# A scan-and-feed-forward layer on one core: the softplus rounding error moves from TensorE to GpSimd, three products instead of four per half, 29 idle products instead of 32, and a new order of work

## The chip, the cores and the metric

The kernel runs on one core of a Trainium2 chip. The metric is the device time of one execution in microseconds (us); three runs of the kernel before took 560.64, 560.69 and 561.02 us, median 560.69. The core has a matrix engine (TensorE, PE), a vector engine (VectorE, DVE), an activation engine (ScalarE, ACT), a general engine (GpSimd, POOL) and a queue for transfers (SyncE, SP). Each runs its own instruction list in order; semaphores make one wait for another.

## The reference

Eight sequences ("images" below) of 512 positions and width 128 go through a Mamba layer and a gated feed-forward layer, each with a residual and a layer norm. Cut to what matters:

```python
h = x * rsqrt(mean(x*x) + 1e-5) * norm_w
xs, res = split(h @ in_proj_w.T)                    # 256 wide each
u = silu(causal_conv4(xs) + conv_b)
delta, Bm, Cm = split(u @ x_proj_w.T, [64, 80])     # 64, 16, 16
delta = softplus(delta @ dt_proj_w.T + dt_proj_b)
# for each of 256 channels and 16 states n, along the 512 positions:
state = exp(delta * A[n]) * state + (delta * u) * Bm[n]
y = sum_n state[n] * Cm[n] + u * D
x = layernorm(x + (y * silu(res)) @ out_proj_w.T + x)
x = layernorm(x + (silu(x @ wg.T) * (x @ wu.T)) @ wd.T)   # hidden 384
```

## The kernel before

**Tiling.** An image's 256 channels times 16 states are 32 groups of 128 rows by 512 positions; 4 groups make a quad, so an image has 8 quads (0 to 7). Quads 0 to 3 belong to channel half 0, quads 4 to 7 to half 1. For each group, ScalarE makes the decay `exp(delta * A)` in one of three PSUM banks (`exp_decay`, L731, up to three groups ahead of the scan, one bank each), and VectorE scans it with `prod` (L1196). GpSimd makes `prod` for a whole quad at once (`multiply`, L1018), into one of two buffers; quad q may be overwritten only when quad q-2 is scanned. After the fourth scan of a quad VectorE weighs the states with the C row (`weigh`, L1206), which TensorE has spread over the partitions in `c_ps` (`spread_c`, "C" in the plan, L484). In five quads of an image (`SHARED`) GpSimd weighs the first group (`weigh_first`, L1040), so that VectorE's weighing covers three groups, not four. TensorE then sums the states into `y_ps` (`sum_states`, "S", L500; at quads 0 and 4 with the skip product L498 ahead of it), and VectorE may not start quad q before the sum of quad q-2 is done.

**What lies beside the scans.** While image k is scanned, the input side of image k+1 ("ins": h, conv, `res`, `xd`, softplus, B rows) and the output side of image k-1 ("outs": projection, first norm, feed-forward, second norm) are worked off in the same loop. TensorE's order is written out by hand: `PLAN` has a list for each quad; "Fname" is an idle product (`stir`, L508, 128x256 on `x_all`, its result is never read) into the bank of the job that it names. `BANK` gives each job one of three PSUM banks; a job and an idle product wait until the bank's job before was taken. `ACT_AT`, `DVE_AT` and `POOL_AT` say after which scan step (0 to 31) or quad the other engines do their part. ScalarE's decay n+1 always comes ahead of its other work of step n.

**The softplus.** `softplus(z)` is `relu(z) + ln(1 + e)` with `e = exp(-|z|)`, and the rounding error of `1 + e` is put back. ScalarE makes `z_abs`, `z_pos` (relu), `z_e`, `z_w = 1 + e`, `z_wm = 1 - z_w` and `z_ln = Ln(1 + e)`; TensorE adds four of them up for each half with products by the identity (job "d": `z_e`, `z_wm`, `z_pos`, `z_ln`; L545 to L551), and ScalarE copies the sum out as `delta` (`take_delta`, L769). SyncE then spreads `delta` and `du = delta * u` (GpSimd, `scale_u`, L1035) over the partitions with 16 transfers for each image. Ln and Silu need other function tables than Exp and Tanh, so ScalarE loads a table ahead of and behind each of them.

**Start and end.** Iteration -1 prepares image 0, iterations 0 to 7 scan an image each (7 has no ins and so none of the idle products named after ins jobs), and `tail` finishes the last image, with idle products of its own (`STIR_TAIL`).

## Time and profile before

| | before |
|---|---|
| median of 3 runs | 560.69 us |
| the profiled execution, its span | 562.91 us, 561.1 us |
| PE busy | 522.8 us (93%) |
| DVE busy | 495.8 us (88%) |
| ACT busy | 385.8 us (69%) |
| POOL busy | 414.2 us (74%) |
| mean granted TensorE clock | 0.963 of 2.4 GHz |

The span runs from the first to the last instruction; the execution's own time is 1.8 us more. A busy TensorE includes the idle products. Most of the span is eight nearly equal stretches, one for each image scanned; each starts with the first scan of the image. A 512-wide fp32 product shows as two records, an idle product as two records, a sum of a quad as eight.

### The profile page before, as it was taken

The page shows a single profiled execution, that of the slowest core. Times are in us where ns is not written, and L with a number is a line of the kernel's source. Part 1 is how long each engine was busy: PE and PEld are TensorE (multiplying, and loading weights), DVE is VectorE, ACT ScalarE, POOL GpSimd, SP SyncE. Part 2 cuts the span into 40 slices and gives each one's busy share as a digit, 9 for nine tenths or more (in the row PEclk, how much of TensorE's full clock was granted, in tenths as well). Part 3 has the DMA queues.
Part 4 walks back from the last instruction along what each step waited for, and adds up shares of the span by engine and source line. Part 5 has one row for each costly group of instructions (what it writes and reads, how often), then busy time and mean ns, then how long its engine had stood idle before and what let it go on. Part 6 is the DMA issues. An engine that isn't in the chain of part 4 may idle for free.

```text
span 561.1 us, 7049 instructions
## 1 busy us (share of the span) xinstructions
PE 522.8 (93%) x2161; PEld 272.9 (49%) x2161; DVE 495.8 (88%) x559; ACT 385.8 (69%) x625; POOL 414.2 (74%) x212
## 2 busy tenths in 40 slices
PE   8989998999999999999999999999999997668695
PEld 6444444545564536545564536544564534433363
DVE  5867789998999999999999999999999999998863
ACT  3676896599478975699478974799478974554231
POOL 8769677996579874996589874996589874996310
PEclk9979999999999999999999999999999999759798
DMA  8062305600624032700624032600634042700000
GB/s 224 9 151 56 96 8 143 151 0 2 150 59 111 1 73 78 167 4 0 151 62 108 0 82 70 169 0 0 150 63 106 0 90 60 168 2 0 0 20 19
DMA packets 27391, 39.29 MB, mean 70 GB/s; under 512 B 3832, under 2 KB 10072, under 8 KB 27360
## 3 DMA queue, kind: packets, MB, share of 16 engines
q1 hardware_dynamic: 25168, 38.38, 28.7%
q10 hardware_dynamic: 2192, 0.55, 0.5%
q8 instruction: 13, 0.21, 0.2%
q14 instruction: 18, 0.15, 0.1%
HBM read 3.27 MB, written 2.10 MB: 10 GB/s over the span
## 4 chain that ended last, share of the span: by engine, by line
PE 74%; DVE 9%; issue 6%; ACT 5%; POOL 2%; DMA 1%; SPq 1%; POOLq 0%; DVEq 0%; ACTq 0%
PE dense_ps L508 18%; PE y_ps L500 9%; PE dense_ps L526 9%; PE dense_ps L577 7%; DVE state L1196 6%; PE dense_ps L584 3%; PE c_ps L484 3%; PE dense_ps L528 2%; PE dense_ps L533 2%; PE dense_ps L545 2%; PE y_ps L498 2%; PE dense_ps L547 2%; PE dense_ps L551 2%; PE dense_ps L549 2%; PE dense_ps L541 2%
## 5 line engine op out<-in xcount | busy, mean ns | idle before, releaser
L1018 POOL TENSOR_TENSOR prod<-du_rep,b_rep 128x2048 f32<-128x2048 f32 x63 | 286.0, 4544 | 71.9 <-ACT b_rep L778 50.0
L1196 DVE TENSOR_TENSOR_SCAN state<-decay_ps,prod 128x512 f32<-128x512 f32 x256 | 298.9, 1207 | 17.3 <-ACT decay_ps L731 10.6
L731 ACT ACTIVATE decay_ps<-delta_rep,a_neg 128x512 f32<-128x512 f32 x252 | 170.0, 689 | 71.8 <-DVE state L1196 71.6
L1206 DVE TENSOR_TENSOR state<-state,c_ps 128x1536 f32<-128x1536 f32 (+1 forms) x63 | 122.8, 1949 | 19.0 <-PE c_ps L484 14.8
L508 PE MATMUL dense_ps<-x_all,ident 128*128 128x256 f32 x476 | 121.8, 398 | 5.6 <-ACT z_pos L757 3.6
L508 PEld LDWEIGHTS dense_ps<-x_all,ident 128*128 128x128 f32 x476 | 88.5, 195 | 48.4 <-issue 15.6
L500 PE MATMUL y_ps<-state,gather 128*32 128x512 f32 x504 | 70.8, 635 | 4.6 <-DVE state L1206 4.6
L526 PE MATMUL dense_ps<-h_t,tap_t 128*128 128x512 f32 x128 | 58.4, 598 | 0.9 <-ACT h_t L789 0.9
L1040 POOL TENSOR_TENSOR state<-state,c_rep 128x512 f32<-128x512 f32 x40 | 51.4, 1285 | 4.3 <-ACT c_rep L774 4.2
L484 PE MATMUL c_ps<-bc,pick 64*128 64x512 f32 x64 | 31.6, 493 | 8.4 <-DVE state L1206 8.4
L526 PEld LDWEIGHTS dense_ps<-h_t,tap_t 128*128 128x128 f32 x128 | 23.2, 189 | 30.5 <-issue 29.4
L1035 POOL TENSOR_TENSOR z_wm<-z_ln,u 128x512 f32<-128x512 f32 x15 | 19.2, 1279 | 23.9 <-ACT z_ln L769 23.8
L484 PEld LDWEIGHTS c_ps<-bc,pick 64*128 64x128 f32 x64 | 12.3, 192 | 36.5 <-issue 22.1
L500 PEld LDWEIGHTS y_ps<-state,gather 128*32 128x32 f32 x504 | 10.1, 110 | 38.1 <-issue 31.7
L577 PE MATMUL dense_ps<-x_t,up_t 128*128 128x512 f32 x42 | 22.2, 651 | 5.3 <-DVE g_act L1271 4.4
L778 ACT ACTIVATE b_rep<-dense_ps 128x512 f32<-128x512 f32 x31 | 17.6, 594 | 9.2 <-PE dense_ps L541 8.9
L577 PE MATMUL dense_ps<-x_t,gate_t 128*128 128x512 f32 x42 | 22.9, 627 | 0.0
L731 ACT ACT_TABLE_LOAD x16 | 20.5, 1283 | 2.4 <-PE decay_ps L477 2.1
L584 PE MATMUL dense_ps<-down_t,g_act 128*128 128x128 f32 x168 | 19.9, 275 | 0.0
L584 PEld LDWEIGHTS dense_ps<-down_t,g_act 128*128 128x128 f32 x168 | 19.3, 192 | 0.0
L769 ACT ACTIVATE z_ln<-dense_ps 128x512 f32<-128x512 f32 x14 | 8.3, 590 | 16.0 <-PE dense_ps L551 16.0
L856 ACT ACTIVATE y_out<-dense_ps 128x512 f32<-128x512 f32 x7 | 4.2, 597 | 21.9 <-PE dense_ps L584 21.9
(201 smaller groups left out, 691.3 us busy)
## 6 DMA issues: line engine op xcount, KB each, us to landing
du_rep<-z_wm SPq DMA_DIRECT2D x64, 256.0 KB, 5.0
delta_rep<-z_ln SPq DMA_DIRECT2D x64, 256.0 KB, 4.5
out_dram<-y_out SPq DMA_DIRECT2D x7, 256.0 KB, 4.7
state<-L_attn_in_proj_w_in ACTq DMA_DIRECT2D x1, 256.0 KB, 3.9
x_all<-L_attn_x_in SPq DMA_DIRECT2D x1, 256.0 KB, 4.2
state<-L_ffn_w_gate_in SPq DMA_DIRECT2D x1, 192.0 KB, 10.0
state<-L_ffn_w_up_in SPq DMA_DIRECT2D x1, 192.0 KB, 3.5
state<-L_ffn_w_down_in SPq DMA_DIRECT2D x1, 192.0 KB, 4.3
```

The lines of the kernel that those rows point to most:

```text
L484: mm(c_ps[:, :], pick[R:, CHUNKS + quad % CHUNKS, :], bc[it.now][R:, :], start=True, stop=True).then_inc(c_ready, 1)
L500: last = mm(y_ps[DB * c:DB * c + DB, :], gather[:, :], state[quad % 2][:, c, :], start=False, stop=(q == CHUNKS - 1), tile_position=(0, DB ...
L508: mm(it.ps(name)[:, 0:2 * P], ident[:, :], x_all[:, 0:2, :], start=True, stop=True)
L526: last = mm(ps[:, :], tap_t[:, n, j, :], h_t[:, j:j + T], start=(j == 0), stop=(j == TAPS - 1))
L577: last = mm(ps[:, :], (gate_t if kind == "gate" else up_t)[:, n, :], x1_t[:, :], start=True, stop=True)
L584: last = mm(ps[:, i * P:(i + 1) * P], g_act[:, b, i * P:(i + 1) * P], down_t[:, b, :], start=False, stop=(b == HID - 1 and i == TILES - 1))
L731: A(decay_ps[n % DECAYS][:, :], decay_ps[n % DECAYS][:, :] if spread_first else delta_rep[:, h, c, :], ACT.Exp, scale=a_neg[:, col:col + 1 ...
L1018: TT(prod[quad % 2][:, :, :], du_rep[:, h, :, :], b, ALU.mult).then_inc(prod_ready, 1)
L1035: TT(du[:, h, :], delta[:, h, :], u[it.next][:, h, :], ALU.mult).then_inc(du_ready, 1)
L1040: TT(state[quad % 2][:, 0, :], state[quad % 2][:, 0, :], c_rep[:, quad % CHUNKS, :], ALU.mult).then_inc(share_ready, 1)
L1196: dve.tensor_tensor_scan(state[n // BLOCKS % 2][:, n % BLOCKS, :], decay_ps[n % DECAYS][:, :], prod[n // BLOCKS % 2][:, n % BLOCKS, :], 0. ...
L1206: TT(state[quad % 2][:, mine, :], state[quad % 2][:, mine, :], c_ps[:, :].unsqueeze(1).broadcast_to([P, BLOCKS - mine.start, T]), ALU.mult ...
```

## The change

GpSimd gets a new step `error_of`: `z_wm = z_e + z_wm`, once for each half. TensorE's job "d" then adds three arrays instead of four, in the order `z_pos`, `z_wm`, `z_ln`. The tables of the order are written anew: the plan has 29 idle products instead of 32, other banks, other steps, and GpSimd takes over the first group in quads 0, 1, 4, 5, 6 instead of 1, 2, 4, 5, 6.

```diff
@@ the plan and the tables (a few of the lines)
-        PLAN = [["Fh", "Fh", "Fh", "Fh", "Fh", "Fh", "Fh", "Fh", "C", "Fh", "S", "h"],
-                ["proj", "xs0", "C", "S", "xs1"],
+        PLAN = [["Fh", "Fh", "Fh", "Fh", "Fh", "Fh", "Fh", "h", "S", "C"],
+                ["Fxs0", "Fxs0", "xs0", "proj", "C", "xs1", "S", "res0", "res1"],
...
-        ACT_AT = {"hx": 1, "y": 4, "h": 3, "r1": 7, "silu": 9, "xd": 13, "x1n": 11, "z": (16, 17), "x1": 16,
-                  "ze": 17, "zw": 19, "zwm": 20, "ln": 21, "gate": (20, 22, 23), "b": (25, 28, 31, 31), "down": 29,
-                  "d": (23, 25), "c": 2}
+        ACT_AT = {"hx": 0, "y": 5, "h": 0, "r1": 5, "silu": 9, "xd": 12, "x1n": 12, "z": (13, 15), "x1": 14,
+                  "ze": 15, "zw": 16, "zwm": 18, "ln": 19, "gate": (19, 19, 21), "b": (24, 28, 31, 31), "down": 28,
+                  "d": (20, 24), "c": 2}
...
-        POOL_AT = {1: [], 2: ["C1"], 3: ["norm1", "C2"], 4: ["low"], 5: ["C4"], 6: ["scale0", "C5"], 7: ["C6"],
-                   8: ["scale1", "norm2"]}
+        POOL_AT = {1: ["C0"], 2: ["C1"], 3: ["norm1"], 4: [], 5: ["low", "error0", "error1", "C4"],
+                   6: ["C5", "scale0"], 7: ["C6", "scale1"], 8: ["norm2"]}
         STIR_HEAD = {"h": 12, "xs0": 3, "du0": 5}
-        STIR_TAIL = {"S": 7, "x1": 6, "gate0": 0}
+        STIR_TAIL = {"S": 8, "x1": 5, "gate0": 1}
@@ TensorE, job "d"
-                    it.wait(pe, z_step, 4, 1, 3)
-                    mm(ps[:, :], ident[:, :], z_e[:, n, :], start=True, stop=False)
-                    it.wait(pe, wm_ready, 1, 1, 1)
+                    it.wait_taken(pe, f"z{n}")
+                    mm(ps[:, :], ident[:, :], z_pos[:, n, :], start=True, stop=False)
+                    it.wait(pe, err_ready, HALVES, 0, n + 1)
                     mm(ps[:, :], ident[:, :], z_wm[:, n, :], start=False, stop=False)
-                    it.wait_taken(pe, f"z{n}")
-                    mm(ps[:, :], ident[:, :], z_pos[:, n, :], start=False, stop=False)
                     it.wait(pe, ln_ready, 1, 1, 1)
                     last = mm(ps[:, :], ident[:, :], z_ln[:, n, :], start=False, stop=True)
@@ GpSimd
+            def error_of(it, h):
+                it.wait(pool, z_step, 4, 1, 3)
+                it.wait(pool, wm_ready, 1, 1, 1)
+                TT(z_wm[:, h, :], z_e[:, h, :], z_wm[:, h, :], ALU.add).then_inc(err_ready, 1)
```

TensorE's list at the start of an image, before, from the sum of the last image's quad 7 (L500) to the first idle products of quad 2; L519 is job h, L556 and L560 are proj, L526 a conv half (xs0, xs1), L528 res0 and res1:

```order
L500 MATMUL y_ps<-state,gather 32x512 x4
L519 MATMUL dense_ps<-ident,hx 128x128 x4
L556 MATMUL dense_ps<-x_all,twice 128x128 x4
L560 MATMUL dense_ps<-out_t,g 128x128 x8
L526 MATMUL dense_ps<-h_t,tap_t 128x512 x4
L484 MATMUL c_ps<-bc,pick 128x512
L498 MATMUL y_ps<-u,skip_t 128x512
L500 MATMUL y_ps<-state,gather 32x512 x4
L526 MATMUL dense_ps<-h_t,tap_t 128x512 x4
L528 MATMUL dense_ps<-h_t,res_t 128x512 x2
L484 MATMUL c_ps<-bc,pick 128x512
```

And the same place now (the line numbers are up to one higher):

```order
L520 MATMUL dense_ps<-ident,hx 128x128 x4
L501 MATMUL y_ps<-state,gather 32x512 x4
L485 MATMUL c_ps<-bc,pick 128x512
L509 MATMUL dense_ps<-x_all,ident 128x256 x2
L527 MATMUL dense_ps<-h_t,tap_t 128x512 x4
L555 MATMUL dense_ps<-x_all,twice 128x128 x4
L559 MATMUL dense_ps<-out_t,g 128x128 x8
L485 MATMUL c_ps<-bc,pick 128x512
L527 MATMUL dense_ps<-h_t,tap_t 128x512 x4
L499 MATMUL y_ps<-u,skip_t 128x512
L501 MATMUL y_ps<-state,gather 32x512 x4
L529 MATMUL dense_ps<-h_t,res_t 128x512 x2
```

Job h now stands ahead of the sum, quad 0's C and two idle products stand between that sum and xs0, xs0 stands ahead of proj, and the sum of quad 0 (with its skip product) stands behind xs1.

ScalarE's list around the logarithm, before; `z_abs` from `z_e` is `z_w`, `g_th` is the Tanh of a gate, and `z_ln` from `dense_ps` is `take_delta`:

```order
L814 ACTIVATE z_abs<-z_e 128x1024
L731 ACTIVATE decay_ps<-delta_rep,a_neg 128x512
L818 ACTIVATE z_wm<-z_abs 128x1024
L847 ACTIVATE g_th<-dense_ps 128x512
L731 ACTIVATE decay_ps<-delta_rep,a_neg 128x512
L827 ACT_TABLE_LOAD
L827 ACTIVATE z_ln<-z_e 128x1024
L731 ACT_TABLE_LOAD
L731 ACTIVATE decay_ps<-delta_rep,a_neg 128x512
L847 ACTIVATE g_th<-dense_ps 128x512
```

And now:

```order
L813 ACTIVATE z_abs<-z_e 128x1024
L730 ACTIVATE decay_ps<-delta_rep,a_neg 128x512 x2
L817 ACTIVATE z_wm<-z_abs 128x1024
L730 ACTIVATE decay_ps<-delta_rep,a_neg 128x512
L826 ACT_TABLE_LOAD
L826 ACTIVATE z_ln<-z_e 128x1024
L846 ACT_TABLE_LOAD
L846 ACTIVATE g_th<-dense_ps 128x512 x2
L730 ACTIVATE decay_ps<-delta_rep,a_neg 128x512
```

The two table loads, the logarithm and two Tanh now stand together between decay 20 and decay 21; before, the loads and the logarithm stood between decay 22 and decay 23, with one Tanh ahead of them and one behind the next decay.

## Rows read from the trace of the kernel before

**Rows 1.** Busy time by image: one of six images, and all six.

```profile
core 0: us, PE busy (x) PEld busy (x) DVE busy (x) ACT busy (x) POOL busy (x), PEclk, DMA share, GB/s
224.84:287.77 62.93, 62.43 (x266) 32.14 (x264) 58.75 (x64) 48.00 (x78) 49.26 (x25) 1.00 0.30 72
...
sum 377.61, PE 370.98 PEld 189.73 DVE 352.62 ACT 285.25 POOL 293.52; mean PE 61.83 PEld 31.62 DVE 58.77 ACT 47.54 POOL 48.92
```

**Rows 2.** Timeline of VectorE in that image: start, us, instruction, [idle before it].

```profile
224.84 2.34 DVE L1196 TENSOR_TENSOR_SCAN state<-decay_ps,prod 128x512 f32<-128x512 f32 x2 [0.71 <-POOL prod L1018]
...
230.14 2.29 DVE L1206 TENSOR_TENSOR state<-state,c_ps 128x2048 f32<-128x2048 f32 x1
...
237.03 1.75 DVE L1206 TENSOR_TENSOR state<-state,c_ps 128x1536 f32<-128x1536 f32 x1
...
243.48 1.22 DVE L1196 TENSOR_TENSOR_SCAN state<-decay_ps,prod 128x512 f32<-128x512 f32 x1 [0.30 <-ACT decay_ps L731]
...
259.82 1.75 DVE L1206 TENSOR_TENSOR state<-state,c_ps 128x1536 f32<-128x1536 f32 x1 [1.37 <-PE c_ps L484]
...
263.21 2.33 DVE L1196 TENSOR_TENSOR_SCAN state<-decay_ps,prod 128x512 f32<-128x512 f32 x2
...
267.65 1.75 DVE L1206 TENSOR_TENSOR state<-state,c_ps 128x1536 f32<-128x1536 f32 x1 [0.40 <-PE c_ps L484]
...
272.70 0.69 DVE L1271 TENSOR_TENSOR g_act<-g_act,dense_ps 128x512 f32<-128x512 f32 x1 [0.44 <-PE dense_ps L577]
...
281.35 0.87 DVE L1296 BATCH_NORM_STATS2 st<-y_out 128x6 f32<-128x128 f32 x4 [0.39 <-ACT y_out L856]
...
284.50 2.29 DVE L1206 TENSOR_TENSOR state<-state,c_ps 128x2048 f32<-128x2048 f32 x1
```

**Rows 3.** Timeline of TensorE in that image.

```profile
225.07 1.07 PE L500 MATMUL y_ps<-state,gather 128*32 128x512 f32 x8
226.07 0.66 PE L519 MATMUL dense_ps<-ident,hx 128*128 128x128 f32 x4
...
240.74 0.50 PE L484 MATMUL c_ps<-bc,pick 64*128 64x512 f32 x1
...
252.22 2.43 PE L508 MATMUL dense_ps<-x_all,ident 128*128 128x256 f32 x10 [0.50 <-ACT z_pos L757]
...
260.61 1.02 PE L545 MATMUL dense_ps<-z_e,ident 128*128 128x512 f32 x2
261.47 1.02 PE L547 MATMUL dense_ps<-z_wm,ident 128*128 128x512 f32 x2
```

**Rows 4.** Timeline of ScalarE in that image.

```profile
242.76 0.69 ACT L731 ACTIVATE decay_ps<-delta_rep,a_neg 128x512 f32<-128x512 f32 x1
...
260.52 1.28 ACT L827 ACT_TABLE_LOAD   x1
261.82 1.06 ACT L827 ACTIVATE z_ln<-z_e 128x1024 f32<-128x1024 f32 x1
...
264.82 0.58 ACT L847 ACTIVATE g_th<-dense_ps 128x512 f32<-128x512 f32 x1
```

**Rows 5.** ScalarE's busy time from decay 11 to decay 23 of that image.

```profile
core 0: us, ACT busy (x), PEclk, DMA share, GB/s
242.76:264.19 21.43, 20.52 (x32) 1.00 0.00 1
```

**Rows 6.** Timeline of GpSimd: an error step of the first image, and a quad's product.

```profile
41.30 1.28 POOL L1022 TENSOR_TENSOR z_wm<-z_e,z_wm 128x512 f32<-128x512 f32 x1 [0.36 <-DVE z_wm L1180]
...
283.12 4.55 POOL L1018 TENSOR_TENSOR prod<-du_rep,b_rep 128x2048 f32<-128x2048 f32 x1 [8.31 <-ACT b_rep L778]
```

**Rows 7.** Timelines of VectorE and TensorE in the first and the last image.

```profile
59.93 1.23 DVE L1196 TENSOR_TENSOR_SCAN state<-decay_ps,prod 128x512 f32<-128x512 f32 x1 [4.19 <-ACT decay_ps L731]
...
490.46 0.79 PE L484 MATMUL c_ps<-bc,pick 64*128 64x512 f32 x1 [3.72 <-DVE state L1206]
...
511.36 1.75 DVE L1206 TENSOR_TENSOR state<-state,c_ps 128x1536 f32<-128x1536 f32 x1 [1.77 <-PE c_ps L484]
```

**Rows 8.** Two stretches of the last image, with the columns of rows 1.

```profile
496.00:506.00 10.00, 8.23 (x27) 4.44 (x29) 9.97 (x8) 6.13 (x12) 9.26 (x3) 0.50 0.01 2
506.00:516.00 10.00, 9.14 (x38) 3.97 (x37) 8.23 (x9) 4.21 (x8) 7.83 (x4) 0.98 0.00 0
```

More of the change, by code:

```diff
@@ L224, in mamba_swiglu_postln @@
         soft_step = sem("soft_step")
+        err_ready = sem("err_ready")
         delta_ready = sem("delta_ready")
@@ L255, in mamba_swiglu_postln @@
         y_free = [sem(f"y_free{i}") for i in range(2)]
-        PLAN = [["Fh", "Fh", "Fh", "Fh", "Fh", "Fh", "Fh", "Fh", "C", "Fh", "S", "h"],
-                ["proj", "xs0", "C", "S", "xs1"],
-                ["res0", "res1", "C", "Fxd", "Fxd", "Fxd", "Fxd", "Fxd", "S"],
-                ["xd", "Fz0", "Fz0", "S", "x1", "Fz0", "Fz0", "z0", "C"],
-                ["z1", "Fgate0", "Fgate0", "Fgate0", "Fgate0", "Fgate0", "S", "Fgate0", "Fgate1", "Fgate1", "Fgate0", "Fgate0", "Fgate1", "gate0", "C", "gate1", "d0"],
-                ["S", "gate2", "C", "d1", "b0"],
-                ["up0", "up1", "up2", "S", "Fb1", "b1", "C", "down", "Fb2", "Fb2"],
-                ["b2", "b3", "C", "S"]]
@@ L266, in mamba_swiglu_postln @@
-        BANK = {"h": 1, "xs0": 1, "proj": 2, "xs1": 0, "res0": 2, "res1": 1, "xd": 2, "z0": 1, "z1": 2, "x1": 0,
-                "gate0": 1, "up0": 2, "gate1": 2, "up1": 0, "gate2": 1, "up2": 2, "b0": 1, "b1": 0, "down": 2,
-                "b2": 0, "b3": 1, "d0": 0, "d1": 0}
-        ACT_AT = {"hx": 1, "y": 4, "h": 3, "r1": 7, "silu": 9, "xd": 13, "x1n": 11, "z": (16, 17), "x1": 16,
-                  "ze": 17, "zw": 19, "zwm": 20, "ln": 21, "gate": (20, 22, 23), "b": (25, 28, 31, 31), "down": 29,
-                  "d": (23, 25), "c": 2}
@@ L272, in mamba_swiglu_postln @@
-        DVE_AT = {"combine": (18, 1), "stats1": 7, "gate": (20, 22, 23), "up": (25, 26, 26), "stats2": 29}
-        POOL_AT = {1: [], 2: ["C1"], 3: ["norm1", "C2"], 4: ["low"], 5: ["C4"], 6: ["scale0", "C5"], 7: ["C6"],
-                   8: ["scale1", "norm2"]}
+        PLAN = [["Fh", "Fh", "Fh", "Fh", "Fh", "Fh", "Fh", "h", "S", "C"],
[7 rows of a table added]
+        BANK = {"h": 1, "xs0": 1, "proj": 0, "xs1": 0, "res0": 2, "res1": 1, "xd": 1, "z0": 2, "z1": 0, "x1": 1,
+                "gate0": 1, "up0": 2, "gate1": 2, "up1": 0, "gate2": 1, "up2": 2, "b0": 1, "b1": 1, "down": 0,
+                "b2": 2, "b3": 1, "d0": 0, "d1": 0}
@@ new lines, in mamba_swiglu_postln @@
+        ACT_AT = {"hx": 0, "y": 5, "h": 0, "r1": 5, "silu": 9, "xd": 12, "x1n": 12, "z": (13, 15), "x1": 14,
+                  "ze": 15, "zw": 16, "zwm": 18, "ln": 19, "gate": (19, 19, 21), "b": (24, 28, 31, 31), "down": 28,
+                  "d": (20, 24), "c": 2}
+        DVE_AT = {"combine": (19, 2), "stats1": 7, "gate": (20, 20, 22), "up": (24, 26, 26), "stats2": 29}
+        POOL_AT = {1: ["C0"], 2: ["C1"], 3: ["norm1"], 4: [], 5: ["low", "error0", "error1", "C4"],
+                   6: ["C5", "scale0"], 7: ["C6", "scale1"], 8: ["norm2"]}
@@ L275, in mamba_swiglu_postln @@
         STIR_HEAD = {"h": 12, "xs0": 3, "du0": 5}
-        STIR_TAIL = {"S": 7, "x1": 6, "gate0": 0}
+        STIR_TAIL = {"S": 8, "x1": 5, "gate0": 1}
         H_FIRST = 3
-        SHARED = [1, 2, 4, 5, 6]
+        SHARED = [0, 1, 4, 5, 6]
         HELD = sorted({quad % CHUNKS for quad in SHARED})
@@ L291, in mamba_swiglu_postln @@
         HEAD_JOBS = ["h", "xs0", "res0", "xs1", "res1", "xd", "z0", "z1", "b0", "du0", "du1", "b1", "b2", "b3"]
-        HEAD_BANK = {**BANK, **{"h": 2, "xs0": 1, "res0": 2, "xs1": 0, "res1": 1, "xd": 2, "z0": 0, "z1": 1, "b0": 2, "du0": 0, "du1": 2, "b1": 0, "b2": 2, "b3": 0}}
+        HEAD_BANK = {**BANK, **{"h": 2, "xs0": 1, "res0": 2, "xs1": 0, "res1": 1, "xd": 2, "z0": 0, "z1": 1, "b0": 2, "du0": 0, "du1": 2, "b1": 0, "b2": 2, "b3": 2}}
         FFN_JOBS = ["gate0", "gate1", "gate2"]
@@ L1091, in iteration @@
                         for h in range(HALVES):
+                            if name == f"error{h}" and it.ins:
+                                error_of(it, h)
                             if name == f"scale{h}" and it.ins:
```

6 rows, old and new, of the table PLAN are left out of this document.

## The prediction

> **What bounds the kernel now.** The span is eight stretches of one image each, so I read one image and multiply. First the busy time by image: the six from the second to the seventh take 62.9 us each, and TensorE is busy for all but half a microsecond of it, VectorE for 58.8, ScalarE for 48, GpSimd for 49 [rows 1]. What the reader is to see is that the idle products make the first of these numbers: 32 of them are in it, and a full TensorE could still be one that is kept busy while it would wait. So the second view is VectorE's timeline with its waits. In one image it stands still for 0.71, 0.30, 1.37, 0.40, 0.44 and 0.39 us [rows 2], 3.6 in all, and four of the six, 2.6 us, wait for TensorE's result (the C row twice, a product of the feed-forward, and the norm's input, which ScalarE copies from TensorE's bank). Third, TensorE's timeline: between all its groups there is a single wait, 0.50 us for `z_pos` [rows 3]; where it makes VectorE wait it is itself late. So both engines stand near the path and TensorE is the one without slack: it cannot finish an image in less than 62.4, VectorE could in 62.9 - 3.6 = 59.3.
>
> **What the change removes and adds.** Two 512-wide products go for each image. The next one starts 0.86 us after the one before [rows 3], so 1.7 us. Three idle products go; ten records, that is five products, take 2.43 us [rows 3] with the modelled end of the last, say 0.45 for one: 1.35 us. TensorE's work falls by 3.1 to about 59.4 us. GpSimd gets two steps of the kind that took 1.28 us in the first image [rows 6]: 2.6 us, 52 of 60 busy. They are on the way to job d, behind `low` and `z_wm`; d needs the logarithm last, and that comes later than the second error step by this count, so they cost nothing while ScalarE is the late one. If that cover were gone, up to 1.3 us would be due once for each image. VectorE's list keeps its length; its weighing of quad 0 now covers three groups (1.75 us) and that of quad 2 four (2.29) [rows 2].
>
> **Where the 3.1 us go.** If nothing else waited, an image would take about 59.5. I follow the new order from the sum of quad 7 (S7) around to the next S7, with the durations of before.
>
> 1. *S7 to scan 11.* Before, S7 starts at 225.07 and `res1` is done when the C product follows at 240.74 [rows 3], 15.7 us. Now h (0.5) is out of this stretch, quad 0's C (0.45) and two idle products (0.95) are in, and xs1 has to wait about 0.3 for ScalarE's copy of proj, whose bank it takes (a copy of this size takes 0.58 [rows 4], the C product covers half): 16.9 us. ScalarE takes both `res` halves in one block with xs, between two table loads, and makes decay 11 only then: 240.74 to scan 11 at 243.48 is 2.74 us [rows 2, 3]. Scan 11 comes at S7 + 19.6; before it came at S7 + 18.4, and VectorE had waited 0.30 for it. The sum of quad 0 behind xs1 now also holds scan 8 for about a microsecond, inside the same delay.
> 2. *Scan 11 to scan 21.* VectorE needed 263.21 - 243.48 = 19.7 us with a wait of 1.37. Without that wait, with 0.54 more for quad 2's weighing and one gate step of 0.6 more, 19.5. ScalarE was busy 20.5 us from decay 11 to decay 23 [rows 5]. The new list has all of that ahead of decay 21, less two decays (1.25), with one Tanh more (0.5, [rows 4]): 19.8 of work without a pause, and about 0.15 to wait for `xd`. Decay 11 starts 0.72 ahead of scan 11 [rows 2, 4], and decay 21 itself has to end, so scan 21 is at scan 11 + 20.0. Here ScalarE is the bound by half a microsecond.
> 3. *Scan 21 to the end of quad 7's weighing.* Before, 263.21 to 284.50 + 2.29 = 286.79 [rows 2], 23.6 us with waits of 0.40, 0.44 and 0.39; one gate step less (0.6). That leaves 21.8, and TensorE by its count reaches each C, gate and up product 0.5 to 3 us ahead of need.
> 4. From there S7 follows in 0.2. The other way around, decay 31, `scale1` (now ahead of the next quad 0's product, 1.28) and the product (4.55 [rows 6]), puts scan 0 some 0.6 later than it could be; the slack up to scan 11 takes that.
>
> The sum is 19.6 + 20.0 + 21.8 + 0.2 = 61.6 us, against 62.9: 1.3 for each of six images, 8 us. TensorE then waits some 2 us in each, in pieces below 1 us. **The first image** has a ScalarE wait of 4.19 at scan 11 [rows 7] whose chain gets two idle products shorter ahead of h and two longer behind; I count nothing. **The last image** loses the wait of 1.77 for quad 5's C row [rows 7], since that now stands behind ten idle products but ahead of the gates; with the 0.7 at its start and smaller ones, 2.2 less. One more idle product ahead of the last sum costs 0.4 in the tail. Total: 8 + 2.2 - 0.4 = 9.8 us off the 562.9 of the profiled execution, 553.1; the median of the runs lies 2.2 below that execution, so 550.9. I take 551.
>
> The step that I size worst is 2, since its pauses are bounded by nothing but the list; if none of the pieces 1 and 2 were late an image would take 59.5, if each were late by 0.7 more it would be back at 63.
>
> **The rivals.** *All of it comes back:* VectorE's floor is met, 59.5 for each image. For it speaks that the order is new throughout and the waits of before go; against it the two counts above, which are hard to avoid. 6 x 3.4 + 1.8 = 22 us less, 539. *It is given back:* the later `res` and the block around the logarithm cost another 1.3 us, or the idle products only stood where TensorE would have waited; an image stays at 62.9, only the last gains: 559. Against it: 2.6 us of VectorE's waits were for a TensorE that did not pause. *The clock falls (slower):* with fewer idle products TensorE pauses ahead of S7, where it waits for ScalarE's `hx` and then for the weighing. In the last image a pause of 3.72 us [rows 7] stands in a stretch whose clock is 0.50, that is 1.2 GHz, and some 8 us of work followed before it was back at 0.98 [rows 8]. It decides from a pause of about that length; I count under 1 us. If it came, 8 us at half speed are 4 lost: an image of 65.6, 6 x 2.7 - 1.8 = 14 more, 575. *A dearer table switch (slower):* both switches now stand in the stretch that I find bound by ScalarE. In the trace, the Ln starts 1.30 us after its table load did [rows 4]. Were each switch dearer by the same again, 2.6 more, an image would take 64.2: 6 us more than before, 567.
>
> The page "ScalarE: Activation LUTs" of the Trainium skill (What ACT_TABLE_LOAD costs) says that a switch to another set costs a drain of some 1.4 us beyond the load, 2.66 in all. By that the stretch would be 2.8 longer. The trace does not agree: 1.30 from load to Ln.
>
> **How the numbers follow.** My forecast 0.71, with a range of its own of 546 to 556; all of it 0.09; given back 0.11; the clock 0.06; the table switch 0.03. The range 542 to 558.5 leaves out most of the first and part of the second rival, and the last two: two in ten. About 0.2%, 1.1 us, is what a measurement tells from no change. Faster: my forecast, the first rival and 0.07 of "given back", 0.87; within 0.2%: the other 0.04; slower: 0.09.
>
> **What would show it.** Images of 61 to 62 us; TensorE busy some 60 of them with waits under 1 us at the sum of quad 7 and the up product; a granted clock of 1.00 in the middle; 1 to 2 us of waiting for ScalarE's decays at scans 11 and 21, next to none for the C row; 1.3 us error steps that nobody waits for; scans still at 1.2 us. Wrong would be a wait of VectorE that I have not listed, above all for the GpSimd product of quad 0 or 1, or a decay behind `x1n`.

## The result and the profile after

The kernel after takes 563.5 us (median of 20 runs, 560.59 to 566.77); the kernel before, run beside it, 560.76 (20 runs, 558.89 to 562.78). The ratio is 1.0054, with a 95% interval of 1.0039 to 1.0068: half a per cent slower, where 551 us had been forecast.

The profiled execution of the kernel after took 560.59 us and was the fastest of its 20; that of before took 562.91, above all 20 of its runs. So the trace after does not show all that a usual run loses, and the two spans (558.6 and 561.1) stand the other way around than the medians. What it shows is where an image is not like its neighbours.

The page of the kernel after, its busy times and granted clock:

```profile
span 558.6 us, 7031 instructions
...
PE 507.9 (91%) x2089; PEld 263.2 (47%) x2089; DVE 497.3 (89%) x559; ACT 389.0 (70%) x625; POOL 431.7 (77%) x226
...
PEclk9989996999999999999999999999999999759899
```

TensorE works 15 us less than before and GpSimd 17.5 more. The clock has a dip in the seventh slice, ahead of 100 us. Busy time by image, the second to the sixth (columns as in [rows 1]):

```profile
100.20:164.42 64.22, 62.56 (x272) 32.32 (x270) 59.16 (x64) 47.20 (x75) 50.22 (x24) 1.00 0.27 63
164.42:226.44 62.02, 60.36 (x262) 31.01 (x254) 58.95 (x65) 48.48 (x79) 51.52 (x27) 1.00 0.31 71
226.44:288.37 61.93, 60.40 (x258) 31.01 (x254) 58.94 (x64) 48.46 (x79) 51.63 (x27) 1.00 0.31 74
288.37:350.44 62.07, 59.80 (x250) 30.35 (x242) 58.95 (x64) 47.63 (x76) 51.61 (x27) 1.00 0.31 73
350.44:415.34 64.90, 61.52 (x262) 31.59 (x266) 59.17 (x65) 49.27 (x81) 51.74 (x27) 1.00 0.30 69
```

Three of the five take 62.0 us, near the forecast 61.6; the second takes 64.2 and the sixth 64.9. From one first scan to the next, over all images, with the images counted from 0 as in the program:

| image | 0 | 1 | 2 | 3 | 4 | 5 | 6 |
|---|---|---|---|---|---|---|---|
| before | 67.35 | 62.95 | 62.85 | 62.93 | 62.84 | 63.14 | 62.91 |
| after | 68.51 | 64.22 | 62.01 | 61.94 | 62.07 | 64.89 | 62.15 |

The last image took 57.3 us from its first to its last scan, before 61.0.

**A steady image.** VectorE's timeline in 288.37 to 350.44, which answers to [rows 2] (start, us, instruction, [idle before it]):

```profile
288.37 3.45 DVE L1202 TENSOR_TENSOR_SCAN state<-decay_ps,prod 128x512 f32<-128x512 f32 x3 [0.74 <-POOL prod L1017]
...
303.16 2.34 DVE L1202 TENSOR_TENSOR_SCAN state<-decay_ps,prod 128x512 f32<-128x512 f32 x2 [0.61 <-PE y_ps L501]
...
307.51 1.22 DVE L1202 TENSOR_TENSOR_SCAN state<-decay_ps,prod 128x512 f32<-128x512 f32 x1 [0.63 <-ACT decay_ps L730]
...
326.44 1.28 DVE L1271 SCALAR_TENSOR_TENSOR g_act<-g_th,dense_ps 128x512 f32<-128x512 f32 x2 [0.26 <-ACT g_th L846]
327.64 2.33 DVE L1202 TENSOR_TENSOR_SCAN state<-decay_ps,prod 128x512 f32<-128x512 f32 x2
...
330.16 0.69 DVE L1271 SCALAR_TENSOR_TENSOR g_act<-g_th,dense_ps 128x512 f32<-128x512 f32 x1 [0.19 <-ACT g_th L846]
...
347.11 2.29 DVE L1212 TENSOR_TENSOR state<-state,c_ps 128x2048 f32<-128x2048 f32 x1
```

The wait of 1.37 for quad 4's C row is gone, as are the 0.40 and 0.44; in their place stand 0.61 for the sum of quad 0, now behind xs1, and 0.63 for decay 11. These are the two waits that the prediction's first piece names.

**Image 5.** It is the first image behind the loop's jump back. ScalarE and TensorE at its start:

```profile
347.82 1.30 ACT L730 ACTIVATE decay_ps<-delta_rep,a_neg 128x512 f32<-128x512 f32 x2 [2.13 <-DVE state L1202]
349.06 0.68 ACT L744 ACTIVATE hx<-x_all,x_rs 128x128 f32 x2
351.54 0.69 ACT L744 ACTIVATE hx<-x_all,x_rs 128x128 f32 x2 [1.80 <-issue]
```

```profile
348.67 1.03 PE L509 MATMUL dense_ps<-x_all,ident 128*128 128x256 f32 x4
352.29 0.66 PE L520 MATMUL dense_ps<-ident,hx 128*128 128x128 f32 x4 [2.59 <-ACT hx L744]
352.88 0.64 PE L501 MATMUL y_ps<-state,gather 128*32 128x512 f32 x4
```

ScalarE stands still for 1.80 us between two of its four `hx` steps, with no releaser ("issue": nothing that the profile shows). It is late before that too: counted from scan 0, its first decay for the new image (the 347.82) starts 1.8 us later than in the image before, and its last `hx` ends 3.2 us later. TensorE waits 2.59 us for `hx`, and the sum of the last image's quad 7, now behind job h, waits with it: scan 4 of the new image may not start before it. The kernel before has the same jump, and its first decay there is 1.8 us late as well, but its four `hx` follow each other without a gap and end only 1.35 us late:

```profile
348.02 1.91 ACT L731 ACTIVATE decay_ps<-delta_rep,a_neg 128x512 f32<-128x512 f32 x3 [2.07 <-DVE state L1196]
349.88 1.31 ACT L745 ACTIVATE hx<-x_all,x_rs 128x128 f32 x4
```

**Images 0 and 1.** TensorE in image 0, and GpSimd ahead of the first of its two long waits:

```profile
76.19 1.12 PE L548 MATMUL dense_ps<-z_wm,ident 128*128 128x512 f32 x2 [2.24 <-POOL z_wm L1033]
...
85.47 0.50 PE L485 MATMUL c_ps<-bc,pick 64*128 64x512 f32 x1 [0.78 <-DVE state L1212]
...
90.07 2.07 PE L509 MATMUL dense_ps<-x_all,ident 128*128 128x256 f32 x4 [2.68 <-ACT b_rep L777]
```

```profile
64.38 9.06 POOL L1017 TENSOR_TENSOR prod<-du_rep,b_rep 128x2048 f32<-128x2048 f32 x2 [6.05 <-DVE state L1202]
73.52 1.26 POOL L990 TENSOR_TENSOR bc<-xd,bc 32x512 fp32r<-32x512 f32 x1
74.86 2.50 POOL L1033 TENSOR_TENSOR z_wm<-z_e,z_wm 128x512 f32<-128x512 f32 x2
```

The error steps stand behind two products of 4.55 us in a row and come 2.2 us late for TensorE. The clock follows; the stretch around the second wait (columns as in [rows 1]), and VectorE's waits in image 0, the last row being the weighing at its end:

```profile
88.00:100.00 12.00, 9.93 (x26) 5.08 (x27) 10.40 (x8) 6.47 (x13) 8.99 (x4) 0.57 0.59 138
```

```profile
50.26 1.75 DVE L1212 TENSOR_TENSOR state<-state,c_ps 128x1536 f32<-128x1536 f32 x1 [1.74 <-ACT c_rep L773]
...
55.04 3.45 DVE L1202 TENSOR_TENSOR_SCAN state<-decay_ps,prod 128x512 f32<-128x512 f32 x3 [3.03 <-PE y_ps L501]
...
59.56 1.22 DVE L1202 TENSOR_TENSOR_SCAN state<-decay_ps,prod 128x512 f32<-128x512 f32 x1 [1.07 <-ACT decay_ps L730]
...
97.43 2.29 DVE L1212 TENSOR_TENSOR state<-state,c_ps 128x2048 f32<-128x2048 f32 x1 [1.28 <-PE c_ps L485]
```

The clock record of the core has half speed (1.2 GHz) from 88.6 for 10.2 us: it falls inside the pause that ends at 90.07. At the lower clock TensorE reaches quad 7's C row late, and the work behind it runs into image 1.

### The profile page after: what moved, and what is told of

Same layout as the page of the kernel before. It is cut to its first block, busy times and chain, and to the rows that moved or that the text cites. A ratio compares the mean times of both kernels' runs of the same rounds, so it can differ in the third digit from the quotient of the medians.

```text
span 558.6 us, 7031 instructions
## 1 busy us (share of the span) xinstructions
PE 507.9 (91%) x2089; PEld 263.2 (47%) x2089; DVE 497.3 (89%) x559; ACT 389.0 (70%) x625; POOL 431.7 (77%) x226
## 4 chain that ended last, share of the span: by engine, by line
PE 64%; DVE 11%; issue 11%; ACT 7%; POOL 4%; DMA 2%; SPq 1%; POOLq 0%; DVEq 0%; ACTq 0%
PE dense_ps L509 14%; PE y_ps L501 9%; PE dense_ps L527 9%; DVE state L1202 7%; PE dense_ps L576 4%; PE dense_ps L583 3%; PE c_ps L485 3%; POOL prod L1017 3%; PE dense_ps L529 2%; PE y_ps L499 2%; PE dense_ps L534 2%; PE dense_ps L559 2%; PE dense_ps L542 2%; ACT x L736 1%; PE dense_ps L579 1%
## 5 line engine op out<-in xcount | busy, mean ns | idle before, releaser
L509 PE MATMUL dense_ps<-x_all,ident 128*128 128x256 f32 x432 | 117.5, 407 | 13.0 <-DVE g_act L1277 9.0
L509 PEld LDWEIGHTS dense_ps<-x_all,ident 128*128 128x128 f32 x432 | 80.3, 198 | 60.4 <-issue 22.4
L501 PE MATMUL y_ps<-state,gather 128*32 128x512 f32 x504 | 69.5, 624 | 5.1 <-DVE state L1212 5.1
L527 PE MATMUL dense_ps<-h_t,tap_t 128*128 128x512 f32 x128 | 58.3, 597 | 1.5 <-ACT r L793 1.5
L485 PE MATMUL c_ps<-bc,pick 64*128 64x512 f32 x64 | 33.1, 517 | 8.9 <-DVE state L1212 8.3
L576 PE MATMUL dense_ps<-x_t,up_t 128*128 128x512 f32 x42 | 21.8, 629 | 0.0
L576 PE MATMUL dense_ps<-x_t,gate_t 128*128 128x512 f32 x42 | 21.8, 627 | 0.0
L846 ACT ACTIVATE g_th<-dense_ps 128x512 f32<-128x512 f32 x21 | 11.9, 596 | 10.7 <-PE dense_ps L576 10.7
L542 PE MATMUL dense_ps<-bc,pick 64*128 64x512 f32 x32 | 16.4, 513 | 2.4 <-ACT b_rep L777 2.2
```

Source lines behind the costliest of these rows:

```text
L485: mm(c_ps[:, :], pick[R:, CHUNKS + quad % CHUNKS, :], bc[it.now][R:, :], start=True, stop=True).then_inc(c_ready, 1)
L501: last = mm(y_ps[DB * c:DB * c + DB, :], gather[:, :], state[quad % 2][:, c, :], start=False, stop=(q == CHUNKS - 1), tile_position=(0, DB ...
L509: mm(it.ps(name)[:, 0:2 * P], ident[:, :], x_all[:, 0:2, :], start=True, stop=True)
L527: last = mm(ps[:, :], tap_t[:, n, j, :], h_t[:, j:j + T], start=(j == 0), stop=(j == TAPS - 1))
L542: last = mm(ps[:, :], pick[R:, n, :], bc[it.next][R:, :], start=True, stop=True)
L576: last = mm(ps[:, :], (gate_t if kind == "gate" else up_t)[:, n, :], x1_t[:, :], start=True, stop=True)
```

## The experiments

Times are medians. Each ratio is to the kernel before, run beside it, with its 95% interval. "Images" are read as in the table above, from one profiled execution, which can stand anywhere in the range of its kernel's times.

**1. The kernel after once more, unedited.** 

> The changed kernel once more, unedited, for its spread and for a second profile. Its 20 runs reach from 560.59 to 566.77 us, and the one profiled is the fastest of them, so its trace (images of 62.0, but 64.2 for image 1 and 64.9 for image 5) does not show what a usual run loses. Theory clock (TensorE's pauses let its clock fall in more places in the usual run): this profile shows one more stretch at a granted clock of 0.50 in the first six images and a span some 3 us longer. Theory loop (ScalarE's list stands still behind the jump back of the loop, 1.80 us in image 5's hx): the clock pattern is the same and the extra time lies at the start of image 5. Ratio to the kernel before 1.004 to 1.007.

561.82 us (559.77 to 566.98, 12 runs), ratio 1.0032 (1.0004 to 1.0059). Images 69.25, 64.37, 62.0, 61.96, 62.04, 65.31, 62.14: the dear ones are again 0, 1 and 5, and this profile is of the median run. In image 5 ScalarE stood for 2.20 us at the same place, and TensorE waited 3.02 us, with its clock at 1.00 before and behind.

**2. The error step and three products alone,** in the old order with its 32 idle products; job d and `error_of` as in the change.

```diff
-        POOL_AT = {... 5: ["C4"], ...}
+        POOL_AT = {... 5: ["C4", "error0", "error1"], ...}
```

> The kernel before with one part of the change alone: the error step on GpSimd and three products for each half, with the old order, banks, steps and all 32 idle products. The error steps stand behind GpSimd's share of quad 4. If TensorE's 1.7 us for each image were on the path, as I predicted (TensorE without slack), the time is 6 to 10 us below that of the kernel before, 551 to 555. If the waits only move (TensorE now waits at quad 5's C and at z_wm), 557 to 561. If the pauses also let the clock fall, above 561.

555.76 us (555.05 to 557.89, 6 runs), ratio 0.9903 (0.9883 to 0.9924). Images 66.11, 62.24, 62.16, 62.22, 62.15, 62.43, 62.21. So 0.7 us in a steady image, not the 1.7 of the two products. VectorE in its steady image:

```profile
319.42 1.75 DVE L1212 TENSOR_TENSOR state<-state,c_ps 128x1536 f32<-128x1536 f32 x1 [1.37 <-PE c_ps L485]
...
327.11 1.75 DVE L1212 TENSOR_TENSOR state<-state,c_ps 128x1536 f32<-128x1536 f32 x1 [0.26 <-PE c_ps L485]
```

The wait of 1.37 for quad 4's C row stands as in [rows 2]: it comes ahead of job d in TensorE's order, and two products fewer behind it cannot shorten it.

**3. The new order with the old start of an image** (29 idle products):

```diff
-        PLAN = [["Fh" x7, "h", "S", "C"],
-                ["Fxs0", "Fxs0", "xs0", "proj", "C", "xs1", "S", "res0", "res1"],
+        PLAN = [["Fh" x8, "C", "Fh", "S", "h"],
+                ["proj", "xs0", "C", "S", "xs1", "res0", "res1"],
-        ACT_AT = {"hx": 0, ..., "h": 0, ...
+        ACT_AT = {"hx": 1, ..., "h": 3, ...
```

> The changed kernel, with the start of an image as before: h behind quad 0's C and the sum of quad 7, proj ahead of xs0, the sum of quad 0 ahead of xs1, hx at step 1 and h at step 3; the number of idle products stays 29. Theory start (the new order there costs: res1 1.2 us later, and h ahead of the sum exposes ScalarE's stall behind the loop's jump): the steady images go from 62.0 to about 61, image 5 loses its extra 2.8, and the time is 8 to 10 us below the changed kernel's. Theory clock: image 5 is as long as the others only by chance, and the time is within 3 us of the changed kernel's.

560.55 us (558.7 to 564.91, 12 runs), ratio 0.9993 (0.9971 to 1.0014). Images 71.54, 62.92, 62.33, 62.11, 62.12, 62.77, 62.21. ScalarE at the start of its image 5:

```profile
352.12 0.39 ACT L744 ACTIVATE hx<-x_all,x_rs 128x128 f32 x1
354.22 0.99 ACT L744 ACTIVATE hx<-x_all,x_rs 128x128 f32 x3 [1.72 <-issue]
```

The same standstill, but job h now stands behind the sum, and image 5 pays 0.7 us for it, not 3. Image 0 is dearer: TensorE waits 3.14 us for `z_wm` and 2.69 for `b_rep`, with 6.8 us at half clock at each of the two. That execution was at the slow end of its twelve.

**4. The kernel after with six idle products at the start of quad 7 in image 0.**

```diff
+                    if it.k0 == 0 and quad == QUADS - 1:
+                        for _ in range(6):
+                            stir(it, "b2")
```

> The changed kernel with six more idle products at the start of quad 7, in image 0 only, where TensorE paused for 2.68 us and its clock fell to 0.50 for 10.2 us (88.64 to 98.88). Theory clock: the clock stays at 1.00 there, image 0 gets 1 us and image 1 2 us shorter (its first TensorE stretch starts late), 3 us in all, so about the time of the kernel before. Theory loop or start: no change of more than 1 us, since the loss is elsewhere.

562.09 us (558.55 to 563.38, 12 runs), ratio 1.0003 (0.9981 to 1.0025). Images 68.54, 61.96, 62.04, 61.96, 62.05, 66.39, 62.14. Image 1 is cured, from 64.2 to 62.0: no half clock at the end of image 0; image 0 itself keeps its 68.5. But image 5 took 66.4. ScalarE's standstill was 1.82 there and TensorE's wait 2.59, as before, yet this time the clock fell. The 4 us behind that pause in this kernel, and under them those in the kernel after:

```profile
350.00:354.00 4.00, 3.87 (x15) 1.53 (x16) 2.03 (x3) 2.12 (x5) 3.81 (x1) 0.57 0.91 231
```

```profile
352.20:356.20 4.00, 3.91 (x20) 2.08 (x21) 2.49 (x4) 3.25 (x7) 3.84 (x1) 1.00 0.95 246
```

A pause of 2.59 us at the same place is followed by half clock in one execution and not in another.

**5 and 6. The loop written out,** once in the kernel after and once with experiment 4's six products as well.

```diff
-            with eng.Fori(0, (B - 4) // 2) as i:
-                for k in (3, 4):
-                    iteration(Iteration(k, 2 * i))
+            for k in range(3, B - 1):
+                iteration(Iteration(k))
```

> The changed kernel with its loop over images 3 to 6 written out, so that no engine jumps back between images 4 and 5; nothing else differs. In both profiles of the changed kernel ScalarE stands still in the middle of hx behind that jump, and image 5 takes 64.9 and 65.3 us where its neighbours take 62.0. Theory loop (the jump back causes the stall, and h ahead of the sum of quad 7 puts it on the path): image 5 is 62.0 to 62.3, about 3 us less in all. Theory clock or chance: image 5 stays near 65.

558.21 us (557.4 to 558.75 in six runs; a seventh, of 1230.08, is left aside), ratio 0.9951 (0.9934 to 0.9968). Image 5: 62.12. Image 1 still 64.89.

> The changed kernel with the loop written out and the six idle products at the end of image 0 as well. If both losses are apart from each other, images 1 to 6 all take 62.0, image 0 still 68.5 or more; the sum against the usual run of the changed kernel is 2.3 + 3 = 5 us, about 557 to 558. If filling only shifts the fall of the clock to a later pause, images 2 to 6 or the last image take it back.

556.16 us (555.47 to 559.75, 7 runs), ratio 0.993 (0.9906 to 0.9954). Images 68.12, 61.97, 62.14, 62.12, 62.12, 62.13, 62.1. With both places mended the change is faster than before, by 0.7%; ScalarE's four `hx` follow each other without a gap in experiment 5, where the jump is gone:

```profile
348.76 1.26 ACT L743 ACTIVATE hx<-x_all,x_rs 128x128 f32<-128x128 f32 x4
351.13 0.69 ACT L787 ACTIVATE h_t<-dense_ps,nw 128x512 f32<-128x512 f32 x1 [1.11 <-PE dense_ps L519]
```

**7. Experiment 2 with the loop written out.** 

> The kernel before with the error step and three products alone, with the loop written out: the control for writing out. In the old order hx stands at step 1 behind three decays and h behind the sum, and the stall behind the jump costs image 5 only 0.2 us (62.43 against 62.2). Theory loop: at most 0.5 us less than with the loop (555 to 556). If writing out itself changed times elsewhere, more than 1 us in either direction.

555.59 us (555.31 to 556.96, 6 runs), ratio 0.9914 (0.9896 to 0.9933), against 0.9903 with the loop. Images 65.98, 62.24, 62.26, 62.23, 62.27, 62.25, 62.23: in the old order the jump costs 0.2 us, in the new one 2.8. In the old order's traces with the loop (the kernel before, experiments 2, 8 and 12) ScalarE is 1.6 to 1.8 us late with its first decay behind the jump, and has no second standstill between its `hx`.

**8. Experiment 2 with three idle products fewer** ahead of gate0 in quad 4's list:

```diff
-                [..., "S", "Fgate0", "Fgate1", "Fgate1", "Fgate0", "Fgate0", "Fgate1", "gate0", "C", "gate1", "d0"],
+                [..., "S", "Fgate0", "Fgate1", "Fgate0", "gate0", "C", "gate1", "d0"],
```

> The kernel before with the error step and three products alone, and then with 29 idle products in the old order: the three that go stand between the sum of quad 3 and gate0, ahead of quad 5's C row, for which VectorE waits 1.37 us in each image. Theory path (idle products ahead of a waited-for C row cost what they take): that wait shrinks to 0.1, a steady image goes from 62.2 to 61.0, and the time from 555.8 to about 547. If ScalarE's block around the logarithm bounds there anyway, 61.5 to 62. Theory clock (fewer idle products let the clock fall): steady images over 63 or an image with a stretch at 0.50.

554.8 us (552.38 to 557.08, 6 runs), ratio 0.99 (0.9872 to 0.9928). Images 66.16, 61.87, 61.81, 61.85, 61.78, 62.1, 61.86. The profiled execution took 552.71. The 1.37, which stood ahead of quad 4's weighing (the expectation says quad 5's), is gone; what comes in its place on VectorE, and on TensorE:

```profile
323.60 0.69 DVE L1271 SCALAR_TENSOR_TENSOR g_act<-g_th,dense_ps 128x512 f32<-128x512 f32 x1 [0.83 <-ACT g_th L846]
```

```profile
319.08 1.13 PE L548 MATMUL dense_ps<-z_wm,ident 128*128 128x512 f32 x2 [0.22 <-POOL z_wm L1033]
...
321.10 1.12 PE L550 MATMUL dense_ps<-z_ln,ident 128*128 128x512 f32 x2 [0.89 <-ACT z_ln L826]
```

1.3 us of idle products give 0.35: behind them ScalarE is the late one. The old order with the change's other parts has a steady image of 61.8, the new order 62.0.

**9 and 10. What holds the new order's image,** each an edit of experiment 6: the sum of quad 0 ahead of xs1, and five instead of seven idle products ahead of h.

```diff
-                ["Fxs0", "Fxs0", "xs0", "proj", "C", "xs1", "S", "res0", "res1"],
+                ["Fxs0", "Fxs0", "xs0", "proj", "C", "S", "xs1", "res0", "res1"],
```

> The changed kernel with the loop written out and image 0 filled (556.2 us, steady images 62.1), and with the sum of quad 0 ahead of xs1 as in the kernel before. VectorE waits 0.61 us for that sum at scan 8 and then 0.63 for decay 11. Theory res (piece 1 of the prediction: scan 11 hangs on res1, whose time this does not change): the first wait goes, the second grows to 1.2, and an image stays at 62.0 to 62.2. If the sum is what counts, 61.5.

554.64 us (553.87 to 556.11, 5 runs), ratio 0.9897 (0.9876 to 0.9917); steady image 61.8. The wait for the sum, 0.38 in experiment 6's steady image, is gone and that for decay 11 has grown from 0.80 there to 0.94. So the sum counts for 0.3, between the two expectations.

```diff
-        PLAN = [["Fh", "Fh", "Fh", "Fh", "Fh", "Fh", "Fh", "h", "S", "C"],
+        PLAN = [["Fh", "Fh", "Fh", "Fh", "Fh", "h", "S", "C"],
```

> The same base with 5 idle products ahead of h instead of 7 (27 in all). Two idle products (0.9 us) still run when hx is ready, so that h starts 0.5 us late and with it the sum of quad 7. If the path goes h, sum of quad 7, xs0, res1, scan 11 (pieces 1 and 4): a steady image takes 61.5 to 61.7, and image 1, behind the slow end of image 0, gains too; 552.5 to 553.5 us. If GpSimd's product of quad 0 holds the start of an image (VectorE waits 0.74 for it): no change, 62.1. Theory clock: fewer idle products bring a fall of the clock at a pause ahead of h, images of 64 and more.

554.95 us (553.75 to 556.47, 6 runs), ratio 0.9902 (0.9882 to 0.9923); steady image 61.8. The 0.9 us of two idle products give 0.3: the wait for the sum of quad 0 is gone here too, decay 11 waits 0.80 as before, and quad 0's product 0.97. TensorE now waits 0.37 for `hx` ahead of job h, so the idle products there no longer hold it up.

**11. Experiment 8 with the loop written out.** 

> The old order with the error step and three products, 29 idle products, and the loop written out: the fastest so far (554.8 with the loop, 552.4 to 557.1) without its loop. Steady images 61.8, image 5 0.3 less; if the runs' spread of 4.7 us comes from the loop it shrinks to 2, around 553; if it comes from where the clock falls in the last image it stays.

555.44 us (552.18 to 556.87, 6 runs: two near 552.2, one of 554.28, three near 556.7), ratio 0.9888 (0.9857 to 0.9919). The profile is of the slowest, with image 0 at 68.47 and image 1 at 63.73. TensorE there, and the windows of the stretch:

```profile
76.60 2.08 PE L547 MATMUL dense_ps<-z_wm,ident 128*128 128x512 f32 x2 [3.26 <-POOL z_wm L1032]
```

```profile
75.00:96.00 21.00, 17.85 (x54) 6.43 (x55) 16.33 (x15) 13.29 (x21) 15.97 (x9) 0.77 0.43 100
```

The wait for GpSimd's error step is in the old order too. Here the clock fell to half at 75.9, inside this wait, and again at 93.0, behind waits of 1.04 us at most, for 6.8 us each. Experiment 8 has the same program up to the loop, and in its profile that wait was 2.54 us, the clock stayed at 1.00, and images 0 and 1 took 66.16 and 61.87: 4.2 us less, about the distance of the two groups. In both experiments the mean granted clock of the runs near 552 is 0.974 and that of the runs near 557 is 0.962.

**12. Experiment 2 without `z_wm` in the sum,** so two products for each half.

```diff
-                    mm(ps[:, :], ident[:, :], z_wm[:, n, :], start=False, stop=False)
```

> The old order with the error step on GpSimd, 32 idle products, and two products for each half instead of three: z_wm, the rounding error, is left out of the sum (job d adds z_pos and z_ln alone), the wait for the error step stays. The first 1.7 us taken off TensorE's list gave 0.7 for each image (62.9 to 62.2). If TensorE were the bound there, another 1.7 would come off, 60.5. If, as the waits of that run show (1.37 for a C row ahead of job d, 0.30 and 0.69 for other engines, 0.26 behind it), what stands behind job d is nearly off the path, an image takes 61.9 to 62.2 and the time is 553.5 to 556.

558.47 us (555.55 to 560.08, 12 runs), ratio 0.9959 (0.9943 to 0.9975). Images 65.46, 63.46, 62.23, 62.26, 62.18, 62.5, 62.26. Two further products fewer give nothing in a steady image; the waits for the C row are 1.37 and 0.30. By the ratios these runs are slower than those of experiment 2, and the profile, of the second fastest of them (556.41), shows it only in part: image 1 takes 1.2 us more, behind a half clock of 3.4 us at 92.6. TensorE's only waits in the 7 us ahead of that fall were 0.46, 0.78 and 0.69 us.

**13 and 14. Image 0 filled ahead of job d,** in experiment 11 and in experiment 9 (which has the six of experiment 4 as well).

```diff
+                            if it.k0 == 0 and name == "d0":
+                                for _ in range(7):
+                                    stir(it, name)
```

> The kernel of e11 (old order, error step, 29 idle products, loop written out; 552.2 to 556.9 us) with seven idle products into the bank of d0, ahead of job d0, in image 0 only, where TensorE paused for 3.26 us and its clock fell to 0.50 twice up to the end of the image. If that pause is the cause of the group at 556.7: images 0 and 1 take 66.1 and 61.9 in every execution and the median is 552 to 553, the spread under 3 us. If the falls come from elsewhere, the two groups stay and the median with them.

552.43 us (552.28 to 554.16, 5 runs), ratio 0.9841 (0.9826 to 0.9856): the fastest. No run is near 556.7. The profile is of the 554.16; its last image took 60.5 us, against 58.2 in experiment 8's. Images 65.43, 61.87, 61.9, 61.89, 61.88, 61.9, 61.88. Its image 0, with the columns of [rows 1]:

```profile
31.00:97.30 66.30, 59.51 (x230) 30.31 (x232) 56.31 (x46) 52.53 (x83) 55.20 (x24) 1.00 0.39 94
```

The clock is 1.00 throughout, and the image takes 0.7 us less than in experiment 8.

> The kernel of e9 (new order, loop written out, sum of quad 0 ahead of xs1, end of image 0 filled; 554.6 us) with the same seven idle products ahead of d0 in image 0. The clock did not fall in that image in e9 (67.99 us), so by the clock theory its time hardly changes, 553.5 to 555; an image 0 shorter by more than 0.5 us would say that the pause itself cost time.

555.54 us (554.63 to 558.42, 5 runs), ratio 0.9915 (0.9893 to 0.9936). Images 69.53, 61.64, 61.8, 61.8, 61.8, 61.8, 61.79; the last 57.19. The steady image equals the old order's; image 0 is 4.1 us dearer. It is also 1.5 us dearer than in experiment 9, so here the seven idle products do harm: the pause for `z_wm` that they fill was 1.06 us in experiment 9 and 3.26 in experiment 11. And the clock did fall in that image in experiment 9, for 3.4 us at 45.3, as it does here at 45.0. Most of the 4.1 us arises there. TensorE in this kernel, and under it in experiment 13:

```profile
44.04 1.14 PE L508 MATMUL dense_ps<-x_all,ident 128*128 128x256 f32 x4 [2.63 <-ACT h_t L793]
45.01 5.29 PE L526 MATMUL dense_ps<-h_t,tap_t 128*128 128x512 f32 x8
50.23 0.49 PE L484 MATMUL c_ps<-bc,pick 64*128 64x512 f32 x1
```

```profile
43.64 3.67 PE L526 MATMUL dense_ps<-h_t,tap_t 128*128 128x512 f32 x8 [1.86 <-ACT h_t L790]
47.24 0.50 PE L484 MATMUL c_ps<-bc,pick 64*128 64x512 f32 x1
```

Quad 1's C row comes 3.0 us later: 1.0 for the two idle products that the new order puts ahead of xs0, 1.6 for xs0 at half clock, 0.4 for a later `h_t`. VectorE waits 3.44 us for it ahead of quad 1's weighing, in experiment 13 0.31.

## Why the prediction was wrong

**The steady image was right but for 0.4 us.** It gained 0.9 us instead of 1.3. Counted in 288.37 to 350.44 against the prediction's pieces:

| piece | predicted | measured |
|---|---|---|
| S7 to scan 11 | 19.6 | 307.51 - 288.01 = 19.5 |
| scan 11 to scan 21 | 20.0 | 327.64 - 307.51 = 20.1 |
| scan 21 to the end of quad 7's weighing | 21.8 | 347.11 + 2.29 - 327.64 = 21.8 |
| from there to S7 | 0.2 | 0.7 |
| image | 61.6 | 62.1 |

The term "from there to S7", 0.2 against 0.7, is mis-sized: idle products still ran when `hx` was ready (experiment 10 took two away and won 0.3). Of the signs, the 1 to 2 us of waiting for decays at scans 11 and 21 came out smaller: 0.63 for decay 11, and ahead of scan 21 only 0.26 for a Tanh.

**The step that failed is "1.3 for each of six images", with "The first image ... I count nothing".** One image was read and multiplied, while the images at the start and behind the loop's jump are other places. In the profiled execution the six gained 0.8 each in four of them and lost it in the other two: 377.3 us together against 377.6 [rows 1], where 369.6 had been forecast. In detail:

- *Image 5:* 2.8 us. ScalarE is late with `hx` behind the jump, and the change put h, which needs it, ahead of the sum of quad 7. Shown from both sides: without the jump 62.1 (experiments 5, 6), with the jump and the old start 62.8 in spite of 1.72 us of standstill (experiment 3). The old order pays only 0.2 us for its jump (experiments 2 and 7): there job h stands behind the sum and the C row and hides the late first decay, but the second standstill, between the `hx`, isn't there at all. Why it comes with the new plan, and in experiment 3 with its old start too, was not found.
- *Image 1:* 2.3 us, by a half clock that began at the end of image 0. Shown by experiment 4, which filled the pause; and by experiments 8 and 11, where images 0 and 1 were 4.2 us dearer with the falls than without, both unfilled (their waits for `z_wm` differ by 0.7 us).
- *Image 0:* 1.2 us against before, but 2.4 against experiment 2 and 3.1 against 13. Its largest wait is 3.03 for the sum of quad 0 behind xs1, and 1.07 for decay 11 follows; the kernel before waits 4.19 for decay 11 alone [rows 7]. With that sum ahead of xs1 (experiment 9) the 4.19 is back and image 0 took 68.0, against 68.1 in experiment 6, so the sum is not the cause. The traces of experiments 13 and 14 put 3.0 us of their difference on quad 1's C row, behind the two idle products ahead of xs0 and a fall of the clock. Experiment 3, with the old start, had image 0 dearer still, but elsewhere: it was level with experiment 2 to within 0.5 us at scan 11 and lost its time from scan 21 to 24, at the wait for `z_wm` and the half clock. How these parts share the cost in the kernel after was not measured by an experiment of its own.

**"GpSimd's error steps cost nothing while ScalarE is the late one"** held in steady images (0.22 us of wait in experiment 8, none in the kernel after) and failed in image 0, where TensorE waited 1.1 to 3.3 us for them. The prediction's bound of 1.3 for the lost cover was too small for that wait: the steps do not only take their own time, they queue behind two products of a quad. What the image pays for it was measured once, in the old order: 0.7 us, from experiment 8 to 13.

**"TensorE is the one without slack"** was half right. It made VectorE wait 1.37 for one C row, but the two products taken away stood behind that place (experiments 2 and 12: 0.7, then 0.0 us). Of 3.1 us off TensorE's list, the old order gives back 1.1 (62.9 to 61.8), and then ScalarE is late. The new order brings nothing beyond that in a steady image.

**The rivals.** *All comes back* (539) is out: even 27 idle products left 61.8. *Given back* (559) came nearest in time, but not by its mechanism: the gains of the steady images are there. *The clock falls (slower)* had the mechanism but not the place: the prediction looked for the pause ahead of S7 in every image and took the 3.72 us of the last one as the length that decides; it came in image 0 and, in one execution, at the jump, with pauses of 2.7 and 2.6, and costs 2.3 us in image 1. I had counted pauses under 1 us, and this held for the steady images alone. Its price was read too low as well: in the kernel before, the half clock of the last image did not end after some 8 us of work, it lasted 17.1 us, from 489.3 to 506.3. And the same trace has a fall at a pause of only 1.66 us, at the start of image 0. *A dearer table switch:* both switches took 1.28 to 1.30 from load to the next ACTIVATE (322.15 to 323.44, 324.52 to 325.81 in the kernel after). The page "ScalarE: Activation LUTs" of the Trainium skill (What ACT_TABLE_LOAD costs) has a drain of some 1.4 beyond the load; nothing here shows it.

**Profiles and medians.** Of the 12.5 us between 551 and 563.5, 7.5 lie between the profiled executions (553.1 forecast, 560.6 measured), and the images account for them: 7.7 in the six, 1.2 in image 0, less 1.5 by which the last gained more than was counted. The other 5 come from where these executions stand: that of before was 2.2 above its median, that of after 2.9 below. The runs' mean granted clock says something of it: 0.964 in the fastest run of the kernel after, 0.961 in those around the median, 0.955 in the five slowest (565.7 us and above). That is, by an estimate from these shares, some 10 us more at half speed in those five than in the first. A further fall in image 5 (66.4 against 64.9 in experiment 4) is one such loss that was seen.

**What stays open.** Where the usual runs lose the rest. The clock alone is not all: runs of the kernel after at one and the same 0.961 reach from 561.7 to 564.5. For the jump as a part of it speaks that writing the loop out gave 4 to 6 us by the ratios (1.0054 or 1.0032 to 0.9951, and 1.0003 to 0.993), more than the 2.8 of the profile after. The last image took 57.2 to 61.4 us between kernels whose parts there are nearly the same. It went with the clock: in the eight profiles where its last fall lasted 3.4 us it took 57.2 to 58.3, in the eight with 6.8 or 10.2 us 58.1 to 61.4. So the 3.7 us that the profile after gains there are not a gain of the change that can be counted on; the prediction had counted 2.2.

## What to carry to other kernels

Read the first image, the last and the one behind a loop's jump with the same care as the steady one before multiplying: two places with 2 to 3 us each took back what four images had gained. A removed product is worth only what the next late engine leaves, and only if it stands ahead of a wait that it causes. Where GpSimd takes over a step, place it by its queue in the fullest image, and where the clock falls at a pause of TensorE, fill that pause in that image alone. In the old order this narrowed the spread of the runs as well (552.2 to 556.9 became 552.3 to 554.2). Fill no more than the pause is long: the same seven products over a pause of 1.1 us made image 0 of the new order 1.5 us longer. And ask which of a kernel's runs the profile shows before two profiles are compared.
